# Last block's attention on the tokens: row sums from ScalarE's accumulator, three float16 products for the values, and new instruction lists

## The reference, cut to what matters

```python
x = _ln(xx, ln1_g, ln1_b)
# in _mha(x, x, ..., causal=True):
xn = _ln(x, lnx_g, lnx_b);  yn = _ln(y, lny_g, lny_b)
q, k, v = (einsum of xn or yn with wq, wk, wv)            # 16 heads of 32
a = jax.nn.softmax(jnp.einsum('bhsd,bhtd->bhst', q, k) * D ** (-0.5), axis=-1)
mask = (jnp.arange(t)[None, :] > jnp.arange(s)[:, None])  # only later keys stay
a = a * mask                                              # after the softmax
o = jnp.einsum('bhst,bhtd->bhsd', a, v)
x_out = x + o @ li1_w + li1_b
```

## Time and profile before

| | us |
|---|---|
| median of 3 runs | 5571.12 (5564.99 to 5577.65) |
| profiled execution | 5523.67 |
| its span, first to last instruction | 5521.9 |
| PE busy | 4866.2 (88%) |
| DVE busy | 3831.6 (69%) |
| ACT busy | 2814.5 (51%) |
| POOL busy | 2176.7 (39%) |

### The profile page before, as it was taken

How to read it: one execution, slowest core, us unless ns; L and a number is a source line. 1 busy time by engine, 2 the same in 40 slices (tenths; PEclk the granted TensorE clock), 3 DMA queues, 4 the chain that set the end, 5 groups by cost and what they waited for, 6 DMA issues and landing times. The chain is left out here.

```text
span 5521.9 us, 132231 instructions
## 1 busy us (share of the span) xinstructions
PE 4866.2 (88%) x41147; PEld 3582.1 (65%) x41147; DVE 3831.6 (69%) x9641; ACT 2814.5 (51%) x6222; POOL 2176.7 (39%) x3095
## 2 busy tenths in 40 slices
PE   7998999999942998899899989999998899998898
PEld 4665668888831565566566667777776677776554
DVE  5786867777765333777777667777767789997444
ACT  4665765555520333455555556666663455554344
POOL 4552001111137000777433357777767433333200
PEclk9998999999965999777999989999999999999978
DMA  1004100000011333100000000000000000000000
GB/s 40 7 10 195 77 1 6 5 5 5 5 65 43 136 135 118 28 23 21 28 1 0 0 6 0 0 0 0 0 1 7 3 2 2 2 2 7 0 14 17
DMA packets 108950, 140.34 MB, mean 25 GB/s; under 512 B 35832, under 2 KB 83257, under 8 KB 103997
## 3 DMA queue, kind: packets, MB, share of 16 engines
q1 hardware_dynamic: 100544, 120.88, 6.4%
q0 software_dynamic: 8192, 16.79, 1.0%
HBM read 47.44 MB, written 58.72 MB: 19 GB/s over the span
## 5 line engine op out<-in xcount | busy, mean ns | idle before, releaser
L2264 POOL TENSOR_TENSOR l3a_probs<-l3a_probs,l3a_later 128x512 f32<-128x512 f32 x256 | 323.9, 1295 | 3.2 <-DVE l3a_total L2456 3.2
L275 ACT ACTIVATE l3a_probs<-l3a_scores,l3a_mx 128x128 f32<-128x128 f32 x1024 | 298.6, 398 | 43.4 <-DVE l3a_mx L249 42.6
L2250 POOL TENSOR_TENSOR l3a_keys<-l3a_kT,head 128x2048 f32<-128x2048 f32 x64 | 230.4, 3600 | 224.9 <-ACT l3a_kT L2381 224.9
L321 PE MATMUL l3a_po<-l3a_vals,l3a_probsT 128*128 128x32 f32 x2048 | 265.9, 274 | 25.7 <-ACT l3a_probsT L302 25.7
L321 PEld LDWEIGHTS l3a_po<-l3a_vals,l3a_probsT 128*128 128x128 f32 x2048 | 251.8, 194 | 43.9 <-ACT l3a_probsT L302 43.9
L2312 PE MATMUL l3a_scores<-l3a_keys,l3a_qT 128*128 128x512 f32 x512 | 268.2, 628 | 4.2 <-POOL l3a_keys L2250 4.2
L181 POOL TENSOR_TENSOR l1x_ve<-l1x_mv,eps 128x1 f32<-128x1 f32 x64 | 12.1, 190 | 647.6 <-DVE l1x_mv L173 647.6
L1747 POOL TENSOR_TENSOR l2f_hid<-l2f_prod,l2f_route 128x512 f32<-128x512 f32 x128 | 152.1, 1193 | 254.3 <-DVE l2f_prod L1894 250.9
L2456 DVE TENSOR_REDUCE l3a_total<-l3a_probs 128x4 f32<-128x512 f32 x256 | 174.6, 682 | 72.9 <-ACT l3a_probs L275 67.8
L1633 PE MATMUL l1e_h<-l1e_xhi,l1f_parts 128*128 128x512 f16 x640 | 204.3, 380 | 9.7 <-DVE l1e_gated L1691 8.2
L2250 POOL TENSOR_TENSOR l3c_keys<-l3c_kT,head 128x1232 f32<-128x1232 f32 x64 | 144.0, 2251 | 157.0 <-ACT l3c_kT L2381 157.0
(11 more groups left out here) (581 smaller groups left out, 16839.8 us busy)
## 6 DMA issues: line engine op xcount, KB each, us to landing
l_rows<-l0f_zeros SPq DMA_DIRECT2D x34, 1024.0 KB, 26.8
l1f_parts<-l1f_split SPq DMA_DIRECT2D x40, 512.0 KB, 3.6
l1e_x_in<-l_rows SPq DMA_DIRECT2D x40, 256.0 KB, 2.8
l1f_down<-l1f_w SPq DMA_DIRECT2D x40, 256.0 KB, 2.4
l_rows<-l1e_y_out SPq DMA_DIRECT2D x40, 256.0 KB, 2.7
l1f_w<-in_L_W SPq DMA_DIRECT2D x16, 256.0 KB, 3.5
out_x<-x_res SPq DMA_DIRECT2D x16, 256.0 KB, 2.0
x_res<-in_x SPq DMA_DIRECT2D x1, 3840.0 KB, 12.3
```

The source lines that it names most:

```text
L275: last = act.activation(self.probs[it.par][:, h, :], self.view(c)[:, h - a, :], ACT.Exp, bias=self.mx[it.par][:, h:h + 1], scale=-1.0)
L321: last = pe.matmul(out_of(h), p[c % 2][:, cols], v, start=(i == 0), stop=(i == len(products) - 1))
L2250: pool.tensor_tensor(keys[it.par][:, :, :, :], kT[it.par][:, :, :].unsqueeze(2).to_broadcast([P, J, G4, T]), g.head32[:, :].unsqueeze(1).u ...
L2264: pool.tensor_tensor(v, v, later[:, :].unsqueeze(1).to_broadcast([P, 4, T]), ALU.mult).then_inc(s_masked, 1)
```

## The change

It has four parts, all for `first=True`.

1. The exponentials of a group write their row sums themselves (`accum_out`), so the DVE's four row sums go. The maskings on POOL and the reciprocal wait for the exponential instead of the sum; the first exponential of a batch waits for the reciprocal of two batches ago.
2. The values are kept as two float16 tiles, `vhi` (scaled, rounded) and `vlo` (the rest), and so are the turned probabilities, `hiT` and `loT`. A head is then three float16 products (hi by hi, hi by lo, lo by hi), added up in PSUM. `fetch_p` and `fetch_v` write float16; DVE computes the remainders `loT` (`remainder`, L307) and `vlo` (`values`, L2449).
3. The next `turn` waits for `vlo`, and the products wait for `loT`.
4. All four engines get new lists, in which each step has its own lag (`placed`).

```diff
+def placed(steps, words):
+    out = []
+    for word in words.split():
+        name, lag = word.split(":")
+        out.append((steps[name][0] if isinstance(steps[name], tuple) else steps[name], int(lag)))
...
             last = act.activation(self.probs[it.par][:, h, :], self.view(c)[:, h - a, :], ACT.Exp,
-                                  bias=self.mx[it.par][:, h:h + 1], scale=-1.0)
+                                  bias=self.mx[it.par][:, h:h + 1], scale=-1.0, accum_out=total[it.par][:, h:h + 1])
...
-        sm = Softmax(st, g, scores, [4] * 4, T, scale, turned, split=not first, direct=first)
+        sm = Softmax(st, g, scores, [4] * 4, T, scale, turned, split=True, direct=first)
...
                 def drop_earlier(it, c):
-                    pool.wait_ge(s_sum, nth(it, 4, c))
+                    pool.wait_ge(sm.s_exp, nth(it, 4, c))
...
-                    names = "spread deviation3 deviation2 deviation1 drop0 drop1 drop2 drop3"
+                    names = ("drop2:5 deviation2:1 drop3:5 drop0:4 deviation1:0 drop1:4 deviation3:1 spread:3")
...
-                    names = ("score0 turn_o turn score1 score2 turn_p0 output queries score3 keys turn_p1 weigh0 turn_p2 weigh1 "
-                             "turn_p3 weigh2 weigh3 values")
+                    names = ("score2:3 output:5 queries:2 turn_p2:4 score3:3 keys:2 weigh0:4 weigh1:4 turn_p3:4 values:2 weigh2:4 "
+                             "weigh3:4 turn_p0:3 turn_p1:3 turn_o:4 score0:2 turn:1 score1:2")
...
-                        act.copy(vals[it.par][:, :], pa[0:T, :]).then_inc(s_vals, 1)
+                    act.activation(vhi[it.par][:, :], pa[0:T, :], ACT.Copy, scale=SPLIT).then_inc(s_vhi, 1)
+                def exponential(it, c):
                     if first:
+                        if c == 0 and (due := nth(it, ago=2)) is not None:
+                            act.wait_ge(s_recip, due)
+                        sm.exponential_of_bank(act, it, c, total)
...
-                    names = "fetch_o fetch_x fetch_p0 exp0 fetch_q exp1 fetch_k fetch_p1 exp2 fetch_p2 exp3 fetch_p3 fetch_v"
+                    names = ("fetch_p3:6 exp2:5 fetch_v:4 fetch_p0:5 exp3:5 fetch_o:6 fetch_x:3 exp0:4 exp1:4 fetch_q:3 "
+                             "fetch_p1:5 fetch_k:3 fetch_p2:5")
...
                 def divide(it):
-                    dve.wait_ge(s_sum, nth(it, 4))
+                    if first:
+                        dve.wait_ge(sm.s_exp, nth(it, 4))
...
-                    names = "hat stats3 maximum0 stats2 maximum1 add sum0 maximum2 sum1 maximum3 stats1 sum2 sum3 divide"
+                    names = ("remainder3:6 stats1:0 divide:6 values:4 hat:2 remainder0:5 maximum0:4 maximum1:4 stats3:1 add:6 "
+                             "maximum2:4 remainder1:5 stats2:0 maximum3:4 remainder2:5")
```

More of the change, by code:

```diff
@@ L67, in first_of, with numbered @@
     return isinstance(it.b, int) and it.b == 0
-def numbered(name, step, count, lag):
+def numbered(name, step, count, lag=None):
     return {f"{name}{c}": (lambda it, c=c: step(it, c), lag) for c in range(count)}
@@ L84, in in_order @@
     return [steps[name] for name in names.split()]
+def placed(steps, words):
[3 more added lines that the diff above has]
+        out.append((steps[name][0] if isinstance(steps[name], tuple) else steps[name], int(lag)))
+    assert len(out) == len(steps)
+    return out
 def nth(it, per=1, c=None, ago=0, back=0):
@@ L2197, in l3_attention @@
         xT, yT = st.sb2("xT", [P, P]), st.sb2("yT", [C, T])
-        qT, kT, vals = st.sb2("qT", [P, J, P]), st.sb2("kT", [P, J, T]), st.sb2("vals", [T, HEADS * D])
+        qT, kT = st.sb2("qT", [P, J, P]), st.sb2("kT", [P, J, T])
         keys = st.sb2("keys", [P, J, G4, T])
-        if not first:
-            vhi, vlo = st.sb2("vhi", [T, HEADS * D], F16), st.sb2("vlo", [T, HEADS * D], F16)
-            s_vhi, s_vlo = st.sem("s_vhi"), st.sem("s_vlo")
+        vhi, vlo = st.sb2("vhi", [T, HEADS * D], F16), st.sb2("vlo", [T, HEADS * D], F16)
+        s_vhi, s_vlo = st.sem("s_vhi"), st.sem("s_vlo")
         total, recip = st.sb2("total", [P, HEADS]), st.sb2("recip", [P, HEADS])
@@ L2273, in _ @@
                     names = "deviation_y spread deviation3 begin_y"
-                skewed(pool, g.B, in_order(steps, names), 8)
+                skewed(pool, g.B, (placed if first else in_order)(steps, names), 8)
             @block.tensor
@@ L2280, in turn @@
                     if (due := nth(it, ago=1)) is not None:
-                        pe.wait_ge(s_vals if first else s_vlo, due)
+                        pe.wait_ge(s_vlo, due)
                     if not first:
@@ L2319, in weigh @@
                     if c == 0:
-                        pe.wait_ge(s_vals if first else s_vlo, nth(it))
+                        pe.wait_ge(s_vlo, nth(it))
                         if (due := nth(it, ago=1)) is not None:
@@ L2324, in values_of @@
                         cols = slice(h * D, (h + 1) * D)
-                        return vals[it.par][:, cols] if first else (vhi[it.par][:, cols], vlo[it.par][:, cols])
+                        return vhi[it.par][:, cols], vlo[it.par][:, cols]
                     sm.times_values(pe, it, c, lambda h: po[:, h * D:(h + 1) * D], values_of)
@@ L2349, in _ @@
                              "weigh1 score3 weigh2 values weigh3")
-                skewed(pe, g.B, in_order(steps, names), 8)
+                skewed(pe, g.B, (placed if first else in_order)(steps, names), 8)
             @block.scalar
@@ L2386, in fetch_v @@
                         act.wait_ge(sm.s_values, due)
+                    act.activation(vhi[it.par][:, :], pa[0:T, :], ACT.Copy, scale=SPLIT).then_inc(s_vhi, 1)
+                def exponential(it, c):
                     if first:
-                        act.copy(vals[it.par][:, :], pa[0:T, :]).then_inc(s_vals, 1)
+                        if c == 0 and (due := nth(it, ago=2)) is not None:
+                            act.wait_ge(s_recip, due)
+                        sm.exponential_of_bank(act, it, c, total)
                     else:
-                        act.activation(vhi[it.par][:, :], pa[0:T, :], ACT.Copy, scale=SPLIT).then_inc(s_vhi, 1)
+                        sm.exponential(act, it, c)
                 def fetch_o(it):
@@ L2460, in divide @@
                     p = it.par
-                    dve.wait_ge(s_sum, nth(it, 4))
+                    if first:
+                        dve.wait_ge(sm.s_exp, nth(it, 4))
+                    else:
+                        dve.wait_ge(s_sum, nth(it, 4))
                     if (due := nth(it, ago=2)) is not None:
@@ L2478, in add @@
                     dve.tensor_tensor(y, po[:, 0:P], y, ALU.add).then_inc(s_out, 1)
-                steps = {**numbered("maximum", lambda it, c: sm.maximum(dve, it, c), 4, 4),
-                         **numbered("sum", row_sum, 4, 4),
+                steps = {**numbered("maximum", lambda it, c: sm.maximum(dve, it, c), 4, 4), "values": (value_remainder, 3),
+                         **numbered("remainder", lambda it, c: sm.remainder(dve, it, c), 4, 5),
                          "hat": (hat, 3 if first else 2), "divide": (divide, 5 if first else 6), "add": (add, 6)}
```

15 lines of the change are left out of this document (7 added, 8 removed).

## The result

The changed kernel takes 5429.9 us (median of 4, 5395.1 to 5443.5), the kernel before 5572.1 beside it: a ratio of 0.973, 95% interval 0.969 to 0.977. Forecast was 5470 in a range of 5395 to 5575. The profiled execution took 5395.1 us (span 5393.3), 128.6 less than that of before.

What follows compares the result with a forecast made beforehand. PE bounded the kernel before on average, not alone; afterwards DVE's 11.57 us of work plus 1.0 of gaps set 12.6 us a batch. (14.18 - 12.6) x 64 batches = 101 us saved, 5571 to 5470 us, range 5395 to 5575.

Steps and rivals of the forecast that it cites:

- Rival D: PE: float16 products don't gain at 128 rows, 0.64 us or more for twelve; 5481 us, within the forecast's chance of 0.54.
- Rival B: ACT: the accumulator read costs 0.26 us a head, making ACT 13.3 us a batch; 5515 us, chance 0.08.
- DVE's sum of 12.6: DVE's own ring per batch: 11.57 us of work, old collisions included, plus 1.0 of gaps.
- Collisions: DVE instructions with SBUF operands held until POOL's current one ends; kept at 1.83 us a batch as before.
- Gaps: Idle time inside DVE's list: 0.44, 0.18, 0.18 and 0.2 too short for the view, 1.0 us a batch.
- Rival A: Fewer collisions on DVE, or they fall into other engines' slack: 165 us saved, 5406 us, chance 0.16.
- ring of 11.6: Loop through PE, ACT and POOL, spread of the keys included: a floor of 11.6 us a batch whatever DVE does.
- sign: What would show the 11.6 us floor deciding: reciprocals 11.6 apart and POOL waiting for the key fetch each batch.
- Rival C: POOL's 3.6 us key spread holds DVE's first hat: 16.4 us a batch, 5713 us (0.14, with overlooked waits); alternating 5560 (0.08).
- point of decision: Which starts first, DVE's first hat (normalization of x_res, about 8.2 us) or POOL's next key spread (8.0 us).
- The argument against it: Late DVE delays scores, hence POOL's spread, more than the first hat: hat at 8.3 us, spread at 9.5.
- two rings: Loops the new lists set: through PE, ACT and POOL, 11.6 us a batch; DVE's own, 12.6 us.

Runs made afterwards that it cites:

- e7: Changed kernel with one float32 product a head for the values and no remainders on DVE, new lists and accumulator kept: 5407.3 us, ratio 0.982, 12.87 us a batch.
- e11: Changed kernel with the row sums back on DVE as four reductions in the new lists, no accumulator: 5591.0 us, ratio 1.006, 14.70 us a batch.
- e6: Kernel before with only the row sums moved to ACT's accumulator, float32 products and old lists kept: 5664.6 us, ratio 1.031, 16.88 us a batch.
- e1: Changed kernel with the bias addition moved from DVE to POOL: 5404.0 us, ratio 0.971, 11.88 us a batch.
- e9: Changed kernel with the bias on POOL and stats1 moved ahead of remainder 1 in DVE's list: 5414.0 us, ratio 0.973, 11.97 us a batch.
- e4: Changed kernel with the row sums left out (no accumulator output, constant 1 written once by POOL): 5702.0 us, ratio 1.025, 16.54 us a batch.
- e2: Changed kernel with DVE's stats2 moved behind remainder 2, into POOL's 3.6 us spread of the keys: 5677.6 us, ratio 1.020, 16.02 us a batch.
- e5: Changed kernel with a short ACT activation writing 1 after each exponential instead of the accumulator: 5336.5 us, ratio 0.970, 11.92 us a batch.
- e10: Changed kernel with the bias on POOL and the row sums left out (constant 1, no accumulator): 5423.2 us, ratio 0.974, 12.15 us a batch.

## Why the prediction was right, and where not

- Float16 products: forecast 0.32 us for twelve, 128 rows no cost; measured 0.305. PE forecast 11.5, measured 11.0 busy. But reading busy PE as the bound before was wrong: its 13.55 us were not all work, since e7 does the same float32 work in batches of 13.00. The slip did no harm, as PE is not the bound in the forecast. Rival D is out.
- Accumulator: forecast 0.10 us a head, measured 0.09; ACT 10.5 busy, forecast 10.8. Rival B is out. The Trainium skill's rule in "VectorE: DVE Perf Modes", section "Two Vector instructions with no wait between them", that an accumulator output makes two instructions, holds on ScalarE too as far as the rows show. The second is recorded with 0.24 us but adds only 0.09. e11 shows what the accumulator is for: with the sums on DVE no gain is left.
- Remainders: 0.683 long, 0.60 apart, as forecast.
- DVE's sum of 12.6 is the term that was mis-sized. Collisions were kept at 1.83 us; measured are 585 - 338, 475 - 338 and 374 - 281 ns (the last by e6's bias row, which met no masking), 0.48 in all. Gaps were put at 1.0; the batch less DVE's busy time is 11.93 - 10.24 = 1.69. Together that is 0.66 less, which is 12.6 less 11.93. So the forecast came as near as it did because two errors of 1.35 and 0.69 us partly cancelled, and that is luck. The gaps left out were 0.21 us ahead of the bias and 0.17 ahead of the reciprocal, and those too short for the view hold 0.46 and not 0.2. That work and gaps add up to the batch is true of any engine and doesn't show that DVE's list sets the pace; e1 shows that it doesn't alone.
- Rival A had the right cause (fewer collisions), and 142 us lies nearer its 165 than the forecast's 101. Its ring of 11.6 was not reached: with the bias moved, a batch still takes 11.88. Nor is its sign there: POOL waits for exponentials (68.5 of 700 us), hardly for the fetch of the keys (1.3). What sets 11.93 stays open. The chain that I read from e1's timelines (divide, turn, ACT's copy and two groups of exponentials, remainder 1, stats2, divide) fits e1 and e9, but no run isolated it.
- Rival C did not happen in this kernel, but its mechanism is there. Its sum said 16.4 us; e4 and e2 have 16.54 and 16.02. Its point of decision, the order of hat and spread, is what e4, e5 and e10 show. The argument against it (DVE's lateness delays the spread more) gave hat and spread 1.2 us apart; the trace has 1.12. The Trainium skill, in "SBUF — State Buffer", section "Who interferes with whom", says that the pair is held exclusively for a whole instruction and that the order of issue decides who is blocked; e4's hat agrees: issued 0.45 us into a spread of 3.60, it took 3.23 where it takes 0.34 alone.
- The parts do not add up. On the old lists each loses 2.7 to 3.3 us a batch, both lose 3.1; the lists are worth 17.23 - 11.93 = 5.3 us with float16 and 4.0 with float32, float16 is worth 0.94 on the new lists. I had treated the lists as a mere setter of two rings.

No run beats the changed kernel beyond its interval: e1 is 3 us faster by its batches (0.05 x 64), which its ratio cannot tell.

## What to carry to other kernels

Where two engines block each other for whole instructions, lay out their order around the longest one and write down the margin: here 1.12 us from start to start carried a gain of 142 us, and taking 1.4 us of work from a third engine turned it into a loss. Judge parts of a reordering change together, since each alone may lose. When a move fills a wait, ask what the moved instruction used to cover.

## What I had not expected of the hardware

A 128x1 activation in place of the accumulator's read costs the same on ACT: from 3300 to 3900 ACT is busy 525.3 us in e5 and 525.5 in the changed kernel, and in both the exponentials start 0.34 us apart. And an engine can be busy 95% of a stage without that being its work: PE's records held 13.7 us of a batch of 14.33 before, and 13.0 in e7, for the same products. The granted clock, 0.98 and 1.00, explains 0.27 of these 0.7; waits such as the 0.17 us shown at e7, which the records cover, account for at least part of the rest. How many there are I didn't count.
